# A recurrent retention stack and a mixture of experts on one core: the gated values' product in f32r parts, in steps with two expert tiles

## What is computed

```
def block(h, p):
    r = _retention(h, wk)
    m = r @ w1 + b1
    a, gate = jnp.split(m, 2, axis=-1)
    m = a * jax.nn.silu(gate) @ w2 + b2
    m = _groupnorm1(m, gg, gb)
    y = m + h
    f = jax.nn.gelu(y @ wf1 + bf1_, approximate=False) @ wf2 + bf2_
    return (_layernorm(f + y, lg, lb), None)
```

## Time and profile before

| | us |
|---|---|
| three runs | 518.02, 518.25, 513.66 |
| their median | 518.02 |
| the profiled execution | 514.47 |
| its span | 512.4 |
| TensorE matmul busy | 475.0 (93%) |
| VectorE busy | 384.8 (75%) |
| ScalarE busy | 253.7 (50%) |
| GpSimd busy | 252.5 (49%) |

### The profile page before, as it was taken

How to read it: one execution, slowest core, us unless ns; L and a number is a source line. 1 busy time by engine, 2 the same in 40 slices (tenths; PEclk the granted TensorE clock), 3 DMA queues, 4 the chain that set the end, 5 groups by cost and what they waited for, 6 DMA issues and landing times.

```text
span 512.4 us, 9849 instructions
## 1 busy us (share of the span) xinstructions
PE 475.0 (93%) x3147; PEld 395.4 (77%) x3147; DVE 384.8 (75%) x1348; ACT 253.7 (50%) x533; POOL 252.5 (49%) x279
## 2 busy tenths in 40 slices
PE   6999889999999999999999999999999999997472
PEld 5887666667888988898889888988888888675242
DVE  4768888878777786677777866777778777888766
ACT  4822434444566655555666555556665544453420
POOL 4520288887545445554454455544444555333341
PEclk9998999999999999999999999999999999999856
DMA  9999411112511111110111111201111000500202
GB/s 265 232 122 222 156 37 38 37 33 78 103 64 58 42 58 42 59 63 32 59 57 44 58 51 48 65 31 59 62 51 46 10 12 12 164 1 1 61 19 84
DMA packets 47345, 35.05 MB, mean 68 GB/s; under 512 B 13320, under 2 KB 38736, under 8 KB 47296
## 3 DMA queue, kind: packets, MB, share of 16 engines
q1 hardware_dynamic: 44496, 28.94, 22.1%
q0 software_dynamic: 2272, 4.71, 2.7%
q10 hardware_dynamic: 528, 0.79, 0.5%
HBM read 14.70 MB, written 9.42 MB: 47 GB/s over the span
## 4 chain that ended last, share of the span: by engine, by line
PE 67%; DVE 12%; POOL 10%; issue 6%; DMA 2%; ACT 2%; POOLq 0%; SPq 0%; DVEq 0%; ACTq 0%
PE bank L1221 9%; PE bank L1148 7%; PE bank L1132 7%; POOL x_slots L471 5%; PE pair L1290 4%; PE pair L1266 4%; PE bank L1303 4%; PE bank L1159 4%; PE pair L1248 4%; PE bank L1160 4%; PE bank L1161 3%; PE pair L1292 3%; PE pair L1246 3%; PE bank L1203 2%; PE bank L1219 2%
## 5 line engine op out<-in xcount | busy, mean ns | idle before, releaser
L483 POOL TENSOR_TENSOR zhat<-zhat,all_lg 128x512 f32<-128x512 f32 x31 | 43.9, 1418 | 88.1 <-PE bank L1193 74.2
L1221 PE MATMUL bank<-all_f,G_sb 128*128 128x128 f32 x512 | 76.8, 284 | 0.0
L651 ACT ACTIVATE y_sb<-bank,gn_bi,gn_sc 128x512 f32<-128x512 f32 x32 | 24.9, 778 | 104.3 <-DVE gn_bi L993 104.2
L1221 PEld LDWEIGHTS bank<-all_f,G_sb 128*128 128x128 f32 x512 | 70.9, 201 | 1.4 <-issue 1.4
L646 ACT ACTIVATE uT_h<-bank 128x512 fp32r<-128x512 f32 x32 | 19.1, 597 | 100.8 <-PE bank L1203 100.8
L426 POOL TENSOR_TENSOR ln_rs<-ln_ve,half_neg 128x4 f32<-128x4 f32 x32 | 33.1, 1033 | 42.0 <-DVE ln_ve L675 41.7
L1132 PEld LDWEIGHTS bank<-moe_w,h_T 128*128 128x128 f32 x312 | 39.5, 191 | 13.9 <-issue 13.9
L498 POOL TENSOR_TENSOR gn_rs<-gn_ve,half_neg 128x1 f32<-128x1 f32 x32 | 18.5, 577 | 58.5 <-DVE gn_ve L888 58.4
L563 ACT ACTIVATE h_T<-bank,w_t 128x128 f32<-128x128 f32 x156 | 44.5, 372 | 5.1 <-PE bank L1148 5.1
L518 POOL DMA_INDIRECT y_rows<-yt,slot_info x39 | 40.9, 1048 | 11.0 <-POOL yt L515 11.0
L631 ACT ACTIVATE G_sb<-bank,all_par 128x512 f32<-128x512 f32 x64 | 43.1, 694 | 5.2 <-PE bank L1184 2.8
(11 more groups left out here) (177 smaller groups left out, 1233.8 us busy)
## 6 DMA issues: line engine op xcount, KB each, us to landing
w_t<-moe_w SPq DMA_DIRECT2D x39, 258.0 KB, 2.4
x_slots<-moe_w SPq DMA_DIRECT2D x1, 2515.5 KB, 20.4
xt<-x_slots SPq DMA_DIRECT2D x39, 64.0 KB, 1.8
x_sb<-in_L_attn_x SPq DMA_DIRECT2D x8, 256.0 KB, 5.7
moe_w<-in_L_ffn_w SPq DMA_DIRECT2D x1, 2048.0 KB, 20.0
moe_w<-y_rows SPq DMA_DIRECT2D x8, 256.0 KB, 4.6
out<-moe_w SPq DMA_DIRECT2D x7, 256.0 KB, 2.4
all_f<-in_L_attn_Wf SPq DMA_DIRECT2D x2, 512.0 KB, 4.2
```

Of the source, the lines that this page charges most:

```text
L483: pool.tensor_tensor(zhat[:, b % 2, :, :], zhat[:, b % 2, :, :], all_lg[:, li, :].unsqueeze(1).broadcast_to([P, C, D]), ALU.mult)\
L1221: last = mm(bank[7][:, at_c], G_sb[:, k, at_c], all_f2[:, li, k, :], start=False, stop=k == 1)
```

## The change

In the 18 steps with two tiles the product with w2 is taken in three f32r matmuls on parts of the gated values and of w2. ScalarE copies gg_sb to gg_h after act_done, and does this ahead of the early tile's gelu. VectorE subtracts it and writes gg_l, directly behind L929. The parts of w2 for layers 1 to 3 are made by GpSimd in step 7, behind the last parts of f1. The new condition in `parted` is true for the same 18 steps as the old one.

```diff
+        gg_h = sb("gg_h", [P, S], f32r)
+        gg_l = sb("gg_l", [P, S], f32r)
+        w2_parts = sb("w2_parts", [P, L - 1, 2, D], f32r)
...
+        PARTS = [("w", 0), ("f1", 0)] + ... + [("w2", l) for l in range(1, L)]
...
-            return turn(l, t, EARLY) is not None and l > 0
+            return turn(l, t, EARLY) is not None and l * B + t > B
...
+            def split_w2(l):
+                split(all_w2[:, l, :], w2_parts[:, l - 1, 0, :], w2_parts[:, l - 1, 1, :])
...
                 if first and t == B - 1:
                     split_f1(L - 1)
+                    for k in range(1, L):
+                        split_w2(k)
... (ScalarE, ahead of the early tile's gelu)
+                if parted(l, t):
+                    act.wait_ge(act_done, l * B + t)
+                    act.activation(gg_h[:, :], gg_sb[:, :], ACT.Copy).then_inc(gg_high, 1)
                 tile_gelu(turn(l, t, EARLY))
... (VectorE, behind L929)
+                if parted(l, t):
+                    dve.wait_ge(gg_high, parted_steps(l, t))
+                    dve.tensor_tensor(gg_l[:, :], gg_sb[:, :], gg_h[:, :], ALU.subtract).then_inc(gg_split, 1)
... (TensorE)
-                    mm(bank[6][:, :], all_w2[:, li, :], gg_sb[:, :], start=True, stop=True).then_inc(pe_w2, 1)
+                    if parted(l, t):
+                        if parted_steps(l, t) == 1 or b == 0:
+                            pe.wait_ge(part_made, parts_made("w2", li))
+                        pe.wait_ge(gg_split, parted_steps(l, t))
+                        parts_product(bank[6], w2_parts[:, li - 1], slice(0, D), gg_h, gg_l, pe_w2)
+                    else:
+                        mm(bank[6][:, :], all_w2[:, li, :], gg_sb[:, :], start=True, stop=True).then_inc(pe_w2, 1)
```

More of the change, by code:

```diff
@@ L210, in retention_moe_kernel @@
         z_half, part_made = sem("z_half"), sem("part_made")
+        gg_high, gg_split = sem("gg_high"), sem("gg_split")
         uT_split, y_high, y_split = sem("uT_split"), sem("y_high"), sem("y_split")
@@ L248, in retention_moe_kernel @@
         LAG = 3
-        PARTS = [("w", 0), ("f1", 0)] + [("w", l) for l in range(1, L)] + [("f1", l) for l in range(1, L)]
+        PARTS = [("w", 0), ("f1", 0)] + [("w", l) for l in range(1, L)] + [("f1", l) for l in range(1, L)] + [("w2", l) for l in range(1, L)]
         def parts_made(what, l):
```

## The result

The changed kernel takes 527.69 us (median of 4 runs, 523.56 to 529.51) against 518.13 us of the kernel before in the same comparison (4 runs). The ratio is 1.019, with a 95% interval of 1.010 to 1.028. The forecast was 526.0 us, slower by 8.0; it is 9.6 by the medians. The profiled execution took 523.56 us with a span of 521.4, 9.0 above that of before.

The account below looks back on a forecast made before the run. TensorE was taken to bound the kernel. 16 x 0.48 = 7.7 us, plus 0.4 in step 28, less 0.1 in step 27, gave 8.0 on the 518.02 us median: 526.0 us, range 515.5 to 531.

Parts of the forecast that it names:

- The mechanism: At w2, gg_l waits for GpSimd's htok operation, ends 0.55 us after it, and TensorE waits; forecast chance 0.65.
- 16 like steps: Steps 9 to 14, 16 to 21 and 23 to 26, alike in timeline; forecast 7.7 us slower in all.
- Case A: Rival: gg_l gets the port before htok or isn't held off; 1.8 us less, 516.2 us; chance 0.2, shared bandwidth included.
- case B: Rival: GpSimd doesn't let VectorE in between htok and the tile's rows; 17.4 us more, 535.4 us; chance 0.1.
- case C: Rival: w2's three f32r matmuls take no less than the plain product; adds 2.9 us, 529 us; chance 0.05.
- The step's size: Late tile's back half starts 0.48 us later in each of 16 steps, TensorE's saving included.
- Step 28: gg_l shut out there by GpSimd's operation on the tile's rows, L515 before the change; adds 0.36 us.
- Step 27: A free step without the stall; given -0.1 us, 0.10 of TensorE's 0.16 us saving being left.
- u's lead: After w2, u is ready only shortly before TensorE wants it; of 0.16 us saved about 0.10 is left.
- What was taken as free: Making w2's parts on GpSimd, gelus and hT behind gg_h on ScalarE, and GpSimd's later tile rows; 0 us.

Follow-up runs that it names:

- PSUM: The changed kernel with the gated values left in PSUM, so gg_l has one SBUF input; ratio 0.998 to the kernel before, steps of 14.67 us.
- the turned order: The changed kernel with GpSimd's htok operation waiting for gg_l, operands still in SBUF; ratio 0.997 to the kernel before, steps of 14.67 us.
- shift of 12: The changed kernel with 12 one-column copies more in VectorE's program, in layer 0; ratio 1.021 to the kernel before, step 28 of 15.05 us.
- shift of 40: The changed kernel with 40 one-column copies more in VectorE's program, in layer 0; ratio 1.025 to the kernel before, step 28 of 13.72 us.

## Why the prediction was right

**The mechanism** in the 16 like steps was as forecast in each part: gg_l just too late for the port (0.07 us behind htok's start, forecast 0.11), its end 0.55 us after htok's, entry ahead of L524, TensorE waiting for gg_l. PSUM and the turned order take the whole loss away, each in its own manner. Case A is excluded by 16 gg_l of 1.74 us, case B by L524's 1.04 us and by gg_l's end, case C by the 0.14 us that a step gains once nothing is in the way.

**The step's size.** 0.53 instead of 0.48 us. From gg_l's end to the weight load it is 0.11 us (255.54 to 255.65), for which I had taken 0.05; the 0.80 us for the product after a wait were right (255.65 to 256.45). That makes 16 x 0.05 = 0.8 us more than forecast.

**Step 28.** I gave it 0.36 us, expecting gg_l to be shut out by L515. It lost 1.48, and in two parts. 1.13 us are y_l behind zhat: so much the step loses when the parts are made and not used (14.53 against 13.40). The other 0.35 are TensorE's wait for gg_l (14.88 against 14.53). That is the size I forecast, by a reason that was partly wrong: gg_l isn't shut out by L515 (0.69 us, also where it begins 0.24 us before that operation's end). From L929's end to w2's weight load there were 1.03 us in this step (426.99 to 428.02) and not 1.85, and the copy and the subtraction need more than that by themselves. Without the shut-out my own sum gives 426.99 + 0.74 + 0.68 = 428.41 for gg_l's end and 0.27 for the step, and 0.32 were measured where y_l was on time.

The term that I had at nothing is the 1.13. I looked only at the new operation's neighbours. y_l's lead over zhat was 0.04 us, and I didn't ask what 18 more instructions on VectorE do to it. That y_l of step 28 begins 0.17 us late is seen in all ten traces with gg_l and no shift, and not in the one without gg_l. The shifts of 12 and 40 show that it isn't gg_l as such, and that the late place moves with the instructions put in ahead; each shift has one trace. Why an instruction is late at such a place is open. The traces have one candidate, which no run tests: a packet of the DMA queue for instructions (q14) begins at 433.11 us in the change, 0.9 after the late y_l, at 430.92 with the shift of 12, 0.4 after the late ln_nb, and at 424.80 with the shift of 40, 7.3 us ahead of ln_nb, and there ln_nb and y_l come on time.

**Step 27 and u.** Step 27 was forecast as free, with 0.10 us of 0.16 left; 0.15 were left. In the other steps it is 0.14 once the port is free. u's lead was right in kind: saving 0.40 rather than 0.16 us on TensorE brought no more.

**What was taken as free** was free: the parts of w2 (GpSimd's zhat began at 134.26 in step 8, at 133.95 before, and step 9 no later than before), ScalarE's queue, GpSimd's rows.

**Luck.** The span grew by 9.0 us and the forecast was 8.0, but the parts lie further apart: 0.8 more in the 16 steps and 1.1 more in step 28, against 0.85 less in the stretches ahead of step 9 and behind step 28, which the mechanism doesn't touch.

## What to carry to other kernels

Where GpSimd and VectorE both work, list VectorE's operations with two SBUF inputs and GpSimd's operations beside them, and look who is first and by how much: being 0.07 us late made an operation 1.06 us longer and each step 0.68 us longer than with the order turned (15.35 against 14.67). An operation that is put in stays cheap at the same place if one input lies in PSUM, or if GpSimd is made to wait for it where it has idle time; cutting GpSimd's operation into pieces bounds the loss. Before changing something to save time on the busiest engine, look how early its next input is ready: here 0.14 us of room bounded any saving on w2.

## What the runs showed of the hardware

- A VectorE operation on 128x512 elements with two SBUF inputs (0.68 or 0.69 us alone) that is shut out by a GpSimd tensor operation ends 0.55 us after that operation's end: gg_l (1.74), y_l (1.69) and the gate's factor (1.17 to 1.46) alike. That is 0.14 us less than it takes alone.
- With one of the two inputs in PSUM it takes 0.69 us beside the same GpSimd operation.
- VectorE, once waiting, gets in between two GpSimd instructions even where GpSimd begins the second one 0.02 us before the first is over (L494 and L524).
- Not every GpSimd instruction shuts VectorE out as long as it lasts. y_sb, with two SBUF inputs, takes 0.69 us in all 32 cases, also inside GpSimd's root on 128x4 elements (1.02 us), and gg_l takes 0.69 where it begins 0.24 us before the end of a 128x128 operation with a scalar (L525). Both rows of the first kind, from the trace of the change:

```profile
429.01 1.02 POOL L430 TENSOR_TENSOR ln_rs<-ln_ve,half_neg 128x4 f32<-128x4 f32 x1 [1.10 <-DVE ln_ve L687]
429.28 0.69 DVE L1018 TENSOR_TENSOR y_sb<-y_sb,hT 128x512 f32<-128x512 f32 x1
```

- VectorE issued y_l 0.17 us late and, after a shift by 12 instructions, ln_nb 0.24 us late, with no wait in the trace that accounts for it (GpSimd's ln_rs, which ln_nb waits for, was over 0.27 us before; without the shift it is 0.03). With a lead of 0.04 us that is enough to turn an order round.
